# Attention: spread the row maxima once per chunk and let VectorE subtract them from every second key block

## The reference, cut to what matters

```python
q = jnp.einsum('bsd,hde->bshe', x, W_Q) + b_Q      # k, v alike
scores = jnp.einsum('bqhe,bkhe->bhqk', q, k) / math.sqrt(D_HEAD)
scores = jnp.where(causal[None, None], scores, -jnp.inf)
pattern = jax.nn.softmax(scores, axis=-1)
z = jnp.einsum('bhqk,bkhe->bqhe', pattern, v)
attn_out = jnp.einsum('bqhe,hed->bqd', z, W_O) + b_O
```

## Time and profile before

| | us |
|---|---|
| median of 3 runs | 2827.72 (2816.59 to 2837.39) |
| profiled execution | 2836.91 |
| its span, first to last instruction | 2835.2 |
| busy TensorE | 2423.6 (85%) |
| busy VectorE | 1909.9 (67%) |
| busy ScalarE | 1200.1 (42%) |
| busy GpSimd | 1152.1 (41%) |

### The profile page before, as it was taken

The page is one execution under the profiler, slowest core; times in us unless marked ns, Lnnn a source line. Parts: engine busy times, 40 slices in busy tenths (PEclk is TensorE's granted clock), DMA queues, the critical chain, the costliest instruction groups (busy, mean ns, idle before and its releaser), DMA issues. The chain is left out here.

```text
span 2835.2 us, 42168 instructions
## 1 busy us (share of the span) xinstructions
PE 2423.6 (85%) x16000; PEld 1223.0 (43%) x16000; DVE 1909.9 (67%) x3874; ACT 1200.1 (42%) x1617; POOL 1152.1 (41%) x781
## 2 busy tenths in 40 slices
PE   3566999999999999999999999305898899888988
PEld 1223555555655555555655554202233232332332
DVE  5864665565656565565656564416989889889988
ACT  3321233333333333333233333104667667666766
POOL 5000375756657575756657574312111211111010
PEclk9788999999999999999999999656999899999999
DMA  1002000000000000000000000560001001000000
GB/s 47 11 23 56 8 1 9 1 9 1 9 23 9 9 1 9 1 9 1 9 3 1 3 1 1 23 80 19 8 18 25 8 18 20 14 18 9 18 7 6
DMA packets 78698, 38.51 MB, mean 14 GB/s; under 512 B 62936, under 2 KB 71192, under 8 KB 77848
## 3 DMA queue, kind: packets, MB, share of 16 engines
q1 hardware_dynamic: 76320, 30.98, 6.4%
q10 hardware_dynamic: 640, 1.69, 0.5%
q0 software_dynamic: 1536, 3.15, 0.4%
HBM read 21.93 MB, written 10.49 MB: 11 GB/s over the span
## 5 line engine op out<-in xcount | busy, mean ns | idle before, releaser
L588 POOL TENSOR_TENSOR acc<-acc,pT 128x1024 f32<-128x1024 f32 (+3 forms) x412 | 829.9, 2014 | 243.6 <-ACT pT L907 210.3
L907 ACT ACTIVATE pT<-banks 128x1024 f32<-128x1024 f32 x480 | 405.7, 896 | 831.1 <-PE banks L661 769.5
L1623 DVE TENSOR_TENSOR hw<-hid,banks 128x512 f32<-128x512 f32 x1024 | 664.1, 679 | 96.1 <-PE banks L1369 85.0
L787 DVE TENSOR_REDUCE part<-banks 128x2 f32<-128x1024 f32 (+3 forms) x432 | 437.9, 1043 | 311.7 <-PE banks L637 310.0
L1496 ACT ACTIVATE hid<-banks 128x1024 f32<-128x1024 f32 x512 | 498.5, 1022 | 271.7 <-PE banks L1359 237.5
L1369 PE MATMUL banks<-wT,select 64*128 64x512 f16 x1024 | 365.0, 413 | 72.3 <-DVE hw L1623 51.4
L677 PE MATMUL banks<-pT,v 128*64 128x512 f32 (+3 forms) x1920 | 405.0, 542 | 1.5 <-POOL pT L576 1.5
L1359 PE MATMUL banks<-zst,w1c 50*128 50x512 f32 x1024 | 330.4, 569 | 5.9 <-ACT hid L1496 4.5
L1377 PE MATMUL banks<-hw,w 128*32 128x512 f32 x2048 | 298.5, 657 | 0.8 <-DVE hw L1623 0.8
L1369 PEld LDWEIGHTS banks<-wT,select 64*128 64x128 f16 x1024 | 96.4, 96 | 462.2 <-DVE hw L1623 368.0
L677 PEld LDWEIGHTS banks<-pT,v 128*64 128x64 f32 x1920 | 116.8, 136 | 202.8 <-issue 180.0
(11 more groups left out here) (183 smaller groups left out, 3051.1 us busy)
## 6 DMA issues: line engine op xcount, KB each, us to landing
zst<-z_scratch SPq DMA_DIRECT2D x48, 128.0 KB, 4.3
z_scratch<-zp SPq DMA_DIRECT2D x8, 512.0 KB, 2.8
out_h<-o SPq DMA_DIRECT2D x8, 384.0 KB, 2.6
xT_scratch<-xs_hi SPq DMA_DIRECT2D x4, 512.0 KB, 2.7
xt_hi<-xT_scratch SPq DMA_DIRECT2D x2, 1024.0 KB, 5.6
w1c<-raw1p ACTq DMA_DIRECT2D x12, 132.0 KB, 5.2
w1c<-raw1p SPq DMA_DIRECT2D x12, 132.0 KB, 4.1
wo<-in_L_attn_W_O SPq DMA_DIRECT2D x12, 96.0 KB, 1.9
```

Of the source, the lines that this page charges most:

```text
L588: pool.tensor_tensor(acc[:, G % 2, :, off:CH], acc[:, G % 2, :, off:CH], pT[:, slot, :, 0:w], ALU.add).then_inc(summed, 1)
L787: last = dve.tensor_reduce(to[:, :, c:c + 1], both[:, :, 0:whole], AX.X, ALU.max)
L907: act.activation(pT[:, J % PSLOTS, :, 0:CH - off], both[:, :, 0:CH - off], ACT.Exp, scale=E ** -0.5)\
L1623: dve.tensor_tensor(hw[:, n % 2, q, :], hid[:, n % 2, q, :], ring_bank(("w", g, n, q)), ALU.mult).then_inc(mixed, 1)
```

## The change

The maxima are no longer spread for each key block. A new item "shifts" per chunk spreads them once: one matmul per head of `ones` by the rows, and ScalarE copies the result into a new SBUF tile `shifts` of two slots (`copy_shifts`). In the order it stands at the end of the sides two macros ahead of the chunk's first block: in macros 0, 4, 10 (chunks 1, 2, 3) and 18 (chunk 0 of the next unit).

Odd key blocks stay as they were, with their spread matmul from `shift_rows`. For even blocks the spread matmul is left out; VectorE adds `shifts` to the scores from PSUM into the `pT` slot (`shift`, at the head of each macro in VectorE's order), and ScalarE takes the exponential there in place. The bank pair of an even block counts as taken when VectorE's addition is done. The waits for a free `pT` slot move to VectorE for even blocks.

```diff
@@ slot_free
-                    pe.wait_ge(TAKEN[prev[0]], nth[prev] + 1)
+                    if prev[0] != "s2":
+                        pe.wait_ge(TAKEN[prev[0]], nth[prev] + 1)
+                    elif prev[2] % 2:
+                        pe.wait_ge(exp_done, prev[1] * NK + prev[2] + 1)
+                    else:
+                        pe.wait_ge(shifted, (prev[1] * NK + prev[2]) // 2 + 1)
@@ sides
+            for Q in range(NQC):
+                unit, t = divmod(it * MACROS + FIRST_OF[Q] - 2, MACROS)
+                if unit == it:
+                    plan[t].append(("shifts", it, Q))
+            if it < LAST:
+                plan[MACROS - 2].append(("shifts", it + 1, 0))
@@ score_columns
-                for h in range(2):
-                    pe.matmul(banks[h][:, 0:w], ones[head(h), :], rows[head(h), u, Q, off:CH], start=True, stop=False)
+                if j % 2:
+                    for h in range(2):
+                        pe.matmul(banks[h][:, 0:w], ones[head(h), :], rows[head(h), u, Q, off:CH],
+                                  start=True, stop=False)
@@ TensorE
+            def spread_shifts(it, Q):
+                banks = slot_free(place[("shifts", it, Q)])
+                pe.wait_ge(rows_copied, it * NQC + Q + 1)
+                for h in range(2):
+                    last = pe.matmul(banks[h][:, :], ones[head(h), :], rows[head(h), it % 2, Q, :],
+                                     start=True, stop=True)
+                last.then_inc(filled, 1)
@@ VectorE
+            def shift(it, j):
+                both = item_in(("s2", it, j))
+                Q, kt, off = key_block(j)
+                J = it * NK + j
+                dve.wait_ge(shifts_copied, it * NQC + Q + 1)
+                if J >= PSLOTS:
+                    dve.wait_ge(pv_done, J - PSLOTS + 1)
+                    wait_summed(dve, *divmod(J - PSLOTS, NK))
+                dve.tensor_tensor(pT[:, J % PSLOTS, :, 0:CH - off], both[:, :, 0:CH - off],
+                                  shifts[:, (it * NQC + Q) % 2, :, off:CH], ALU.add).then_inc(shifted, 1)
...
             for it in range(UNITS):
                 for t in range(MACROS):
+                    shift(it, 2 * t)
                     for item in PLAN[it][t]:
                         side(item)
@@ ScalarE, exponentials
+                to = pT[:, J % PSLOTS, :, 0:CH - off]
+                if j % 2 == 0:
+                    act.wait_ge(shifted, J // 2 + 1)
+                    act.activation(to, to, ACT.Exp, scale=E ** -0.5).then_inc(exp_done, 1)
+                    return
@@ ScalarE
+            def copy_shifts(it, Q):
+                both = item_in(("shifts", it, Q))
+                G = it * NQC + Q
+                if G >= 2:
+                    unit, chunk = divmod(G - 2, NQC)
+                    act.wait_ge(shifted, shifts_before(unit * NK + LASTKEY[chunk]))
+                act.activation(shifts[:, G % 2, :, :], both, ACT.Copy).then_inc(shifts_copied, 1)
```

More of the change, by code:

```diff
@@ L421, in stage_attention @@
         mask = sb("mask", [P, P])
+        shifts = sb("shifts", [P, 2, 2, CH])
         part = sb("part", [P, 2, TQ * 2, COLS])
@@ L430, in stage_attention @@
         max_taken, c_ready, rows_copied = sem("max_taken"), sem("c_ready"), sem("rows_copied")
+        shifts_copied, shifted = sem("shifts_copied"), sem("shifted")
         exp_done, masked, summed = sem("exp_done"), sem("masked"), sem("summed")
@@ L442, in stage_attention @@
         TAKEN = {"q": low_taken, "k": low_taken, "v": v_taken, "s1": max_taken, "rows": rows_copied,
-                 "s2": exp_done, "total": total_copied, "out": out_added}
+                 "shifts": shifts_copied, "total": total_copied, "out": out_added}
+        FIRST_OF = [min(j for j, (Q, _) in enumerate(KEYS) if Q == q) // 2 for q in range(NQC)]
         def first_pass(n):
@@ L483, in stage_attention @@
         PLAN = [sides(it) for it in range(UNITS)]
-        order = first_pass(0)
+        order = first_pass(0) + [("shifts", 0, 0)]
         for it in range(UNITS):
@@ L496, in stage_attention, with shifts_before @@
             counts[name] = nth[item] + 1
+        def shifts_before(J):
+            return (J + 1) // 2
         def two_banks(m):
@@ L651, in score_columns @@
                 Q, kt, off = key_block(j)
-                if kt == 0:
-                    pe.wait_ge(rows_copied, it * NQC + Q + 1)
                 w = CH - off
                 t0 = Q * CH + off
-                for h in range(2):
-                    pe.matmul(banks[h][:, 0:w], ones[head(h), :], rows[head(h), u, Q, off:CH], start=True, stop=False)
+                if j % 2:
+                    for h in range(2):
+                        pe.matmul(banks[h][:, 0:w], ones[head(h), :], rows[head(h), u, Q, off:CH],
+                                  start=True, stop=False)
                 terms = ((kh, qh), (kh, ql), (kl, qh))
@@ L661, in score_columns @@
                         last = pe.matmul(banks[h][:, 0:w], a[head(h), u, kt * P:(kt + 1) * P],
-                                         b[head(h), u, t0:t0 + w], start=False, stop=(k == 2))
+                                         b[head(h), u, t0:t0 + w], start=(k == 0 and j % 2 == 0), stop=(k == 2))
+                last.then_inc(filled, 1)
[5 more added lines that the diff above has]
+                                     start=True, stop=True)
                 last.then_inc(filled, 1)
@@ L712, in side @@
                     output(*item[1:])
+                elif item[0] == "shifts":
+                    spread_shifts(*item[1:])
                 else:
@@ L718, in _ @@
                 side(item)
+            spread_shifts(0, 0)
             for it in range(UNITS):
@@ L857, in side @@
                     take_v(*item[1:])
-                elif item[0] != "rows":
+                elif item[0] not in ("rows", "shifts"):
                     take_low(*item)
@@ L901, in exponentials @@
                 J = it * NK + j
+                Q, kt, off = key_block(j)
+                to = pT[:, J % PSLOTS, :, 0:CH - off]
[3 more added lines that the diff above has]
+                    return
                 both = item_in(("s2", it, j))
-                Q, kt, off = key_block(j)
                 if J >= PSLOTS:
@@ L906, in exponentials @@
                     wait_summed(act, *divmod(J - PSLOTS, NK))
-                act.activation(pT[:, J % PSLOTS, :, 0:CH - off], both[:, :, 0:CH - off], ACT.Exp, scale=E ** -0.5)\
-                   .then_inc(exp_done, 1)
+                act.activation(to, both[:, :, 0:CH - off], ACT.Exp, scale=E ** -0.5).then_inc(exp_done, 1)
+            def copy_shifts(it, Q):
[5 more added lines that the diff above has]
+                act.activation(shifts[:, G % 2, :, :], both, ACT.Copy).then_inc(shifts_copied, 1)
             def copy_total(it, Q):
@@ L919, in side @@
                     copy_rows(*item[1:])
+                elif item[0] == "shifts":
+                    copy_shifts(*item[1:])
                 elif item[0] in "qk":
@@ L924, in _ @@
                 side(item)
+            copy_shifts(0, 0)
             for it in range(UNITS):
```

## The result

The changed kernel takes 3085.5 us (median of 4 runs, 3083.1 to 3086.6). Against the kernel before the ratio is 1.091 (95% interval 1.087 to 1.096): 9% slower. The profiled execution has a span of 3083.3 us.

The account below looks back on a forecast made before the run. TensorE was taken as the bound, nearly without a gap. Profiled 2836.9 us, plus 168 for eleven units (18.4 of stalls less 3.15 saved in each), 33 for the last unit and 4, gave 3042, at the median 3033; range 2950 to 3115.

Parts of the forecast that it names:

- TensorE's saving: Even blocks' spread matmuls: net 168 full pairs fewer at 0.225 us, 37.8 us less, 3.15 us in a unit.
- TensorE's slack of 0.10 us in the third item: Third side item starts 0.10 us after B's banks are free, so eight wide macros each lose 1.28 us.
- The addition: VectorE's 240 additions for even blocks: 1.22 us each at full width, 0.69 at 512 elements, 267 us in all.
- that rival: Additions collide with GpSimd: 0.8 us more in each of 13 macros and in the last unit, 3150 us; chance 0.04.
- The exponential from SBUF: exp(A) on ScalarE, now reading SBUF instead of PSUM: taken as no change in time.
- The late additions: Macros 9, 14, 15: VectorE still inverts or normalises when A is filled; net stalls 2.35, 3.8 and 2.4 us.
- The clock: Rival: TensorE, less busy in attention, falls to clock 0.92; plus 80 us, 3113 us; chance 0.09.
- its step fails below 0.97 in attention: Failure sign: the forecast's step fails if the granted clock of attention lies below 0.97.
- one stretch, from 270 to 285 us: Evidence against the clock rival: TensorE busy 11.39 of 15 us with short gaps, at clock 1.00.
- The new items: Once-per-chunk spreading: in macros 4 and 10 it becomes third item, 2.6 us together; in macros 0 and 18 no wait.
- The last unit: Without sides, addition, exponentials and odd sum form a loop: 5.9 us per full macro instead of 3.93; plus 33 us.
- the 9 us that the forecast took off: Median of the three runs before lay 9.2 us below the profiled execution, so 3042 became 3033.

Follow-up runs that it names:

- the experiment where nothing else waits: Kernel before, without the even blocks' spread matmuls and nothing in their place, and with three VectorE inversions moved to the head of earlier macros: 2765.7 us, ratio 0.974.
- half the addition: Changed kernel, with VectorE adding only one head of each even block: 3037.2 us, ratio 1.072.
- work in the gaps: Changed kernel, with the matmuls of two side items repeated inside the waits of macros 9 and 14: 3061.3 us, ratio 1.082.
- the exponential done twice: Kernel before, with ScalarE doing each even block's exponential twice, the first time into a spare tile: 2963.7 us, ratio 1.045.
- the experiment: Changed kernel, with its last unit as before (no additions or once-per-chunk spreading there, spread matmuls for every block): 3048.8 us, ratio 1.075.
- first experiment: Kernel before, without the spread matmuls of the even key blocks and with nothing in their place: 2812.1 us, ratio 0.993.
- inversions moved on the changed kernel: Changed kernel, with three VectorE inversions and a normalising moved from the end of macros 7, 8 and 13 to their head: 3061.8 us, ratio 1.081.

## Why the forecast was right, and where it was short

The direction and the mechanism held. 3033 was forecast with 2950 to 3115, and 3085.5 came, just above the forecast's own narrower range of 2990 to 3080.

**TensorE's saving.** 0.225 us a pair was right: -0.20 to -0.24 in macros 1, 2 and 13, which have only it (macro 3, with two projections and an output, gained nothing), and 3.9 us a unit in the experiment where nothing else waits. TensorE's slack of 0.10 us in the third item was read rightly too: 17, 12 and 8 came out at 1.05, 1.05 and 1.20 for 1.05.

**The addition.** 1.22 us by L773, 1.223 measured; GpSimd doesn't slow it (1.21 to 1.23 us for all 192), and its sums stay at their 2.37. As a price on each addition that rival is out. But VectorE does lose time to GpSimd elsewhere: the small cast that closes the maxima waits for a running sum, up to 2.3 us, and the additions queued behind it are late. The exponential from SBUF was taken as no change and costs 0.03 to 0.05 us.

**The late additions** were sized at 3.8, 3.8 and 2.4 us of waiting in macros 9, 14 and 15. Macro 9 waits 3.00. In macro 14 of the same unit the two waits are 1.37 and 1.04; in macro 15 only 1.35 remain, for exp(B). The step that failed is the one that kept VectorE's lateness fixed at what the trace of before shows. In macro 14 the inversion began 1.80 us behind the first score matmul of A, and 1.58 of that were the cast waiting for GpSimd; in the change the cast began 0.3 us later in the macro, near the end of a sum, and took 0.30, so the inversion began at 0.85. That was a coincidence of the two queues, as half the addition shows, where the cast takes 2.32. In macro 15 the lateness is nearly gone since TensorE itself waited in macro 14, and VectorE caught up meanwhile; with work in the gaps, where macro 14 is 1.6 us shorter, TensorE's wait for the addition grows from 0.12 to 0.88. In lengths, with the clock's 2.3 and 1.6 us taken off macros 9 and 14, the three come out 0.2 above the forecast, 0.9 below and 1.5 below: 2.2 us a unit too high.

**The clock** was left out of the sum and had a chance of 0.09. It is the main miss: some 4 us a unit, 3.9 by the kernel with work in the gaps, and more in the last unit, where the mean is 0.81 and was 0.93. By the forecast's own sign (its step fails below 0.97 in attention) this step failed: 0.96. (Its price had a slip too: 1368 us of busy time at 0.92 grow by 119, not 109.) The argument against it was one stretch, from 270 to 285 us, with TensorE busy 76% in short gaps at the full level. No kernel here changes that stretch. In the trace of the changed kernel it reads (columns as above):

```profile
270.00:285.00 15.00, 12.23 (x80) 7.29 (x76) 13.63 (x35) 0.60 (x1) 0.00 (x0) 0.89 0.00 0
```

In seven of the twelve traces the clock falls there. The 1.00 of one execution was luck, and no evidence. The length of one wait doesn't decide either. These are macro 6 of two neighbouring units of the changed kernel, each with one wait of 1.34 us for exp(B):

```profile
503.44:511.97 8.53, 6.96 (x46) 4.12 (x44) 4.03 (x8) 2.46 (x3) 3.39 (x2) 0.80 0.00 0
650.71:657.66 6.95, 5.38 (x46) 3.33 (x44) 4.04 (x8) 2.46 (x3) 3.31 (x2) 1.00 0.00 0
```

The clock falls in macro 6 in two of the eleven units, and these are the two in which it takes 8.53 us and not 6.95; of its 0.46 us above the forecast, 0.35 are that. The rule of the Trainium skill that was put beside this rival ("TensorE: Matmul & The Clock Gate", "A second HAM failure mode: psum-queue depth-cycling") was the better guide here: TensorE idled as it cycled through its PSUM banks, and the clock went down and up in macros 9 and 14 of every unit. It doesn't say when, though: with the exponential done twice TensorE waited over 120 times in 1200 us, for up to 1.1 us, at a clock of 1.00.

**The new items.** Macro 0 was forecast at nothing and costs 1.40: the once-per-chunk item, in second place, needs A's banks (0.30 us of waiting for the addition), and the total that follows the weighting needs B's (0.48). The step that failed looked only at the third side item and took the weighting as cover; two of the blocks weighted there are narrow, 0.87 us in all. Macros 4 and 10 were short by 0.3 each, mostly the transition to the new matmul (its pair takes 0.43 us up to the weighting and not 0.225). Together 2 us a unit too low, macro 6's 0.5 not included.

**The last unit** was right in its sum: plus 33 forecast, 31 in the trace (137.4 for 106.7), 32 in the experiment. In part that is luck: three of the twelve full loops hold a copy of 0.69 us in place of a sum of 2.65, and the lower clock, put at nothing, lies in it as well.

Summed by the table: 2.2 too much for lateness, against 3.9 for the clock, 2.0 for the new items, 0.5 for macro 6 and 0.5 for all other macros together: 4.6 or 4.7 us a unit short. Eleven times that is the 52 us by which the eleven units missed (220 us more, 168 forecast). That the totals also miss by 52 is chance: in the profiled executions the last unit came out 2 us lower and the stage behind attention 6 us lower than forecast, and the 9 us that the forecast took off, because the profiled execution of before lay above its median, did not come again.

What stays open: how much of the last unit's loss is clock (by estimate at most some 19 us, 0.19 of 139.9 less 0.07 of 106.7, if TensorE never idled); and why, behind the same waits, the clock falls in some units and not in others.

## What to carry to other kernels

When a bound engine waits for buffers, what counts is the time from "filled" to "free" on a chain of in-order queues, not the busy share of any engine on it: an operation put in front of one consumer also delays the consumer queued behind it. So put new work in front of the block whose buffers are needed last, and read the slack between "free" and "due" from the timeline before moving anything. A wait on TensorE costs its own length and, in some units here and not in others, also the clock of what follows, so one stretch of one trace at full clock is no proof that it stays up; a stall filled with useless matmuls can be cheaper than an empty one. And when an operation of VectorE is read as long in a trace, look at what GpSimd does at that moment before carrying its length into a forecast: the same small cast took from 0.17 to 2.32 us.

## What the runs showed of the hardware

- TensorE fell to the lower clock level behind waits of 2.50 us in every unit, in nine of eleven before the next wait and in two after it (changed kernel, macro 9), of 1.90 in seven of eleven (first experiment), of 1.34 in two of eleven (changed kernel, macro 6) and of 1.04 in four of eleven (inversions moved on the changed kernel, macro 9). It did not behind 1.45 us (before, clock 1.00 through the eleven units) nor in 1200 us with waits up to 1.1 us and a busy share of 93% (the doubled exponential). Which units it hits isn't explained by the length of the wait. At the lower level eight matmuls of the weighting took up to 3.35 us for 1.94, the output 2.93 for 1.57.
- VectorE's cast of 128x8 from SBUF to SBUF took 0.17 us beside an idle GpSimd; in twelve traces 354 such casts that met a running operation of GpSimd ended 0.03 to 0.04 us behind it, up to 2.33 us long.
- Repeating 3.4 us of matmuls a unit made the changed kernel 24 us faster (28 in attention).
- VectorE's addition of a PSUM and an SBUF tile of 1024 elements took 1.223 us on the mean of 192, with GpSimd busy 56% of the stretch on SBUF, no longer than without it.
- ScalarE's exponential of 1024 elements took 1.058 us from SBUF and 1.006 from PSUM when it followed another without a gap.
